# An attention and mixture-of-experts block: in the second half of the program, TensorE's products of one kind are put together

## What is computed

```python
x = x + _layernorm(_L0_attn_ref(_layernorm(x), Wq, bq, Wk, bk, Wv, bv))
x = x + _layernorm(_L0_ffn_ref(_layernorm(x), W_enc, ..., ln_g, ln_b))

# _L0_attn_ref
scores = jnp.einsum('bqh,bkh->bqk', q, k) / scale
probs = jax.nn.softmax(scores, axis=-1)
return jnp.einsum('bqk,bkh->bqh', probs, v)

# _L0_ffn_ref: D=128, H=256, M=64, E=8 experts, K=2 of them used, EH=128
spikes_enc = jax.nn.sigmoid(inputs_embeds @ W_enc + b_enc)
cont = flat @ W_s2c + b_s2c
probs = jax.nn.softmax(cont @ Wr + br, axis=-1)
topk_w, topk_idx = jax.lax.top_k(probs, K)
...
h = jax.nn.relu(jnp.einsum('tm,emh->eth', cont, W1) + b1[:, None, :])
y = jnp.einsum('eth,ehm->etm', h, W2) + b2[:, None, :]
expert_out = jnp.einsum('etm,te->tm', y, gate)
spikes_moe = jax.nn.sigmoid(expert_out @ W_c2s + b_c2s)
return _layernorm(spikes_moe @ W_dec + b_dec, ln_g, ln_b)
```

## Time and profile before

| | before |
|---|---|
| median of 3 runs | 129.09 us |
| the profiled execution | 128.96 us |
| its span, first to last instruction | 127.1 us |
| PE busy | 120.1 us, 94% |
| DVE busy | 91.7 us, 72% |
| ACT busy | 60.5 us, 48% |
| POOL busy | 34.7 us, 27% |

### The profile page before, as it was taken

One profiled execution on the slowest core, in us unless ns is written; L12 is line 12 of the kernel. 1 busy time (PEld: TensorE's weight loads), 2 busy tenths in 40 slices (PEclk: granted clock), 3 DMA queues, 4 the chain that ended last, 5 costly groups with the idle time before them and its releaser, 6 DMA issues.

```text
span 127.1 us, 2496 instructions
## 1 busy us (share of the span) xinstructions
PE 120.1 (94%) x814; PEld 80.0 (63%) x814; DVE 91.7 (72%) x390; ACT 60.5 (48%) x179; POOL 34.7 (27%) x71
## 2 busy tenths in 40 slices
PE   6999999999999999999999999999999999999940
PEld 2756785769638677755466776765548755864830
DVE  0858986996379625689765855899775986979873
ACT  1557765548646486303548662012552432281830
POOL 4422635232222003304000034402321311343361
PEclk9999999999999999999999999999999999999997
DMA  3548810000000039400000394002940029802022
GB/s 118 136 102 229 217 57 0 0 0 3 0 5 0 5 111 365 189 8 0 0 0 5 115 376 179 0 5 86 410 179 0 2 81 352 313 9 83 3 85 83
DMA packets 9371, 12.43 MB, mean 98 GB/s; under 512 B 3169, under 2 KB 5998, under 8 KB 9358
## 3 DMA queue, kind: packets, MB, share of 16 engines
q1 hardware_dynamic: 8782, 12.14, 27.9%
q10 hardware_dynamic: 576, 0.13, 0.5%
HBM read 11.16 MB, written 1.11 MB: 97 GB/s over the span
## 4 chain that ended last, share of the span: by engine, by line
PE 70%; DVE 11%; ACT 5%; DMA 4%; POOL 3%; issue 2%; POOLq 1%; SPq 0%; DVEq 0%
PE ps_o L826 11%; PE ps_s L801 10%; PE ps_t L934 7%; PE ps_t L813 5%; PE ps_s L913 4%; PE ps_ac L913 4%; POOL rstd L436 3%; PE ps_o L852 3%; DMA gate_all<-gates 3%; PE ps_ac L852 3%; PE ps_ac L774 2%; PE ps_ac L870 2%; PE ps_ac L784 2%; PE ps_t L752 2%; DVE gated L1304 2%
## 5 line engine op out<-in xcount | busy, mean ns | idle before, releaser
L436 POOL TENSOR_TENSOR rstd<-var_eps,minus_half 128x2 f32<-128x2 f32 (+1 forms) x32 | 24.9, 779 | 82.6 <-DVE var_eps L1188 41.3
L826 PEld LDWEIGHTS ps_o<-v,probsT 128*128 128x128 f32 x128 | 15.5, 192 | 4.8 <-ACT probsT L554 4.8
L826 PE MATMUL ps_o<-v,probsT 128*128 128x128 f32 x128 | 17.7, 281 | 0.3 <-ACT probsT L554 0.3
L934 PE MATMUL ps_t<-gated,w 128*64 128x256 f32 x128 | 17.1, 390 | 0.0
L549 ACT ACTIVATE probs<-ps_s,neg_max 128x512 f32<-128x512 f32 x16 | 11.0, 687 | 11.9 <-DVE neg_max L1211 11.8
L801 PE MATMUL ps_s<-xnT,yT 128*128 128x512 f32 x32 | 16.2, 600 | 0.0
L1211 DVE TENSOR_REDUCE neg_max<-ps_s 128x1 f32<-128x512 f32 x16 | 11.0, 690 | 5.5 <-PE ps_s L801 5.4
L934 PEld LDWEIGHTS ps_t<-gated,w 128*64 128x64 f32 x128 | 7.9, 136 | 7.4 <-DVE gated L1304 2.5
L1304 DVE SCALAR_TENSOR_TENSOR gated<-ps_s,b_minus,gate_all 128x512 f32<-128x512 f32 x14 | 10.0, 745 | 2.9 <-PE ps_s L913 2.2
L554 ACT ACTIVATE probsT<-ps_t 128x512 f32<-128x512 f32 x16 | 9.5, 594 | 2.6 <-PE ps_t L813 2.5
L813 PEld LDWEIGHTS ps_t<-ident,probs 128*128 128x128 f32 x64 | 7.3, 141 | 4.6 <-ACT probs L549 2.5
(11 more groups left out here) (203 smaller groups left out, 220.2 us busy)
## 6 DMA issues: line engine op xcount, KB each, us to landing
gate_all<-gates SPq DMA_DIRECT2D x12, 512.0 KB, 6.2
gate_all<-gates SPq DMA_DIRECT2D x8, 256.0 KB, 3.5
x_in<-in_L_attn_x SPq DMA_DIRECT2D x3, 256.0 KB, 3.6
w<-in_L_ffn_W SPq DMA_DIRECT2D x3, 256.0 KB, 4.3
out<-x_out SPq DMA_DIRECT2D x3, 256.0 KB, 2.0
x_in<-in_L_attn_x SPq DMA_DIRECT2D x2, 128.0 KB, 2.4
out<-x_out SPq DMA_DIRECT2D x2, 128.0 KB, 1.7
w_enc<-in_L_ffn_W_enc SPq DMA_DIRECT2D x1, 128.0 KB, 2.3
```

The lines of the kernel that those rows point to most:

```text
L436: nc.gpsimd.tensor_tensor(rstd[part], var_eps[part], minus_half[:, t0:t1], ALU.pow).then_inc(g_rstd[n], 1)
L826: mm = nc.tensor.matmul(attn_out(t), probsT[:, b % 2, t, k], v[:, b % 2, k], start=(k == 0), stop=(k == T - 1))
L934: mm = nc.tensor.matmul(ps_t[h * M:(h + 1) * M, 0:SH], w2[:, e], gated[:, e, h * SH:(h + 1) * SH], start=False, stop=(e == E - 1))
```

## The change

In the list of PE the work from batch 3's attention on is written in another order, so that products of one kind stand next to each other more often. `encode(2)` and `hidden_pair(1, 0)` go into batch 3's attention; `to_spikes(0)` goes behind it. The four tiles of a decode stand together, as do two pairs of hidden units and four or six expert sums. The lists of ACT and DVE follow. DVE's additions to the logits become two instructions for each batch, one for each bank; the logits of batch 2 lie in `ps_t` and `ps_a` in place of `ps_c`. Each expert sum raises `pe_moe` by one, so that `gate_hidden(b, e)` waits for the sum of the same expert of the batch before and no longer for all eight. One edit is earlier in the program: on ACT, `pT_out(1, 1)` goes ahead of `exps(1, 2)`. No product, activation or transfer is added or removed other than the four additions.

```diff
-        def logit_banks(b):
-            return ps_c if b in (0, 2) else ps_o
+        def logit_bank(b, h):
+            if b == 2:
+                return ps_a if h else ps_t
+            return (ps_o if b % 2 else ps_c)[:, h]
...
@@ ACT's list
+            pT_out(1, 1)
             exps(1, 2)
-            pT_out(1, 1)
...
@@ expert_out(b, e)
-                if e == E - 1:
-                    mm.then_inc(pe_moe, 1)
+                mm.then_inc(pe_moe, 1)
...
@@ PE's list, from the expert sums of batch 1 on
             hidden_pair(1, 1)
-            decode(0, 0)
-            decode(0, 1)
             hidden_pair(1, 2)
-            expert_out(1, 2)
-            expert_out(1, 3)
-            decode(0, 2)
-            decode(0, 3)
+            for t in range(T):
+                decode(0, t)
+            for e in range(2, 6):
+                expert_out(1, e)
             hidden_pair(1, 3)
...
             hidden_pair(2, 1)
             route(3)
-            decode(1, 0)
-            decode(1, 1)
-            expert_out(2, 2)
+            for t in range(T):
+                decode(1, t)
             hidden_pair(2, 2)
-            decode(1, 2)
-            decode(1, 3)
             hidden_pair(2, 3)
-            expert_out(2, 3)
-            expert_out(2, 4)
-            expert_out(2, 5)
+            for e in range(2, E):
+                expert_out(2, e)
             hidden_pair(3, 0)
-            expert_out(2, 6)
-            expert_out(2, 7)
             hidden_pair(3, 1)
             to_spikes(2)
             expert_biases(3)
+            expert_out(3, 0)
+            expert_out(3, 1)
             decode_part(2, 0)
             hidden_pair(3, 2)
-            expert_out(3, 0)
-            expert_out(3, 1)
             hidden_pair(3, 3)
...
@@ gate_hidden(b, e), DVE
-                if e == 0 and b >= 1:
-                    dve.wait_ge(pe_moe, b)
+                if b >= 1:
+                    dve.wait_ge(pe_moe, E * (b - 1) + e + 1)
...
@@ DVE's list, near the end
             dec_var(1, 0)
-            gate_hidden(3, 0)
-            gate_hidden(3, 1)
+            for e in range(4):
+                gate_hidden(3, e)
             z_scale(1, 0)
             z_stats(1, 0)
             z_means(1, 0)
-            for e in range(2, E):
+            dec_scale(2, 0)
+            for e in range(4, E):
                 gate_hidden(3, e)
-                if e == 3:
-                    dec_scale(2, 0)
```

More of the change, by code:

```diff
@@ L689, in _ @@
             pT_out(3, 0)
-            spike2(0, 0)
-            spike2(0, 1)
+            spike(2, 0)
             exps(3, 2)
@@ L993, in decode @@
                     pe.wait_ge(a_c2s, HC * (b + 1))
-                if t == 0:
-                    pe.wait_ge(a_cont, b + 3)
+                if b == 0 and t == 0:
+                    pe.wait_ge(v_logit, 2 * (B - 1))
+                elif t == 0:
+                    pe.wait_ge(a_cont, B)
                 last = any(t == t1 - 1 for _, t1 in parts(LN_DEC, b))
@@ L1101, in _ @@
             turn_h(2)
-            to_spikes(0)
             turn_probs(3, 0)
             scores(3, 2)
+            encode(2, 0)
             attend(3, 0)
@@ L1107, in _ @@
             scores(3, 3)
+            encode(2, 1)
             attend(3, 1)
             turn_probs(3, 2)
-            encode(2, 0)
+            hidden_pair(1, 0)
             attend(3, 2)
             turn_probs(3, 3)
-            encode(2, 1)
+            to_cont(2)
             attend(3, 3)
-            hidden_pair(1, 0)
-            to_cont(2)
+            route(2)
+            to_spikes(0)
             expert_biases(1)
             expert_out(1, 0)
-            route(2)
             expert_out(1, 1)
             hidden_pair(1, 1)
-            decode(0, 0)
-            decode(0, 1)
             hidden_pair(1, 2)
-            expert_out(1, 2)
-            expert_out(1, 3)
-            decode(0, 2)
-            decode(0, 3)
+            for t in range(T):
+                decode(0, t)
+            for e in range(2, 6):
+                expert_out(1, e)
             hidden_pair(1, 3)
-            expert_out(1, 4)
-            expert_out(1, 5)
             hidden_pair(2, 0)
+            turn_h(3)
             expert_out(1, 6)
             expert_out(1, 7)
-            turn_h(3)
+            encode(3, 0)
+            encode(3, 1)
             to_spikes(1)
             expert_biases(2)
-            encode(3, 0)
-            encode(3, 1)
             expert_out(2, 0)
@@ L1506, in _ @@
             attn_var(3, 0)
+            gate_hidden(1, 0)
+            gate_hidden(1, 1)
             mid_stats(3, 0)
-            gate_hidden(1, 0)
-            attn_var(3, 1)
-            gate_hidden(1, 1)
             router_top(2)
             router_index(2)
+            router_gates(2)
+            attn_var(3, 1)
             gate_hidden(1, 2)
-            gate_hidden(1, 3)
-            router_gates(2)
-            gate_hidden(1, 4)
-            gate_hidden(1, 5)
             mid_stats(3, 1)
+            for e in range(3, 6):
+                gate_hidden(1, e)
+            mid_norm(3, 0)
+            mid_norm(3, 1)
             gate_hidden(1, 6)
             gate_hidden(1, 7)
-            mid_norm(3, 0)
-            mid_norm(3, 1)
             dec_var(0, 0)
```

50 lines of the change are left out of this document (28 added, 22 removed).

## The result

The changed kernel took 130.78 us as the median of nine runs (129.95 to 132.9), the kernel before 129.06 us in as many. The ratio is 1.0121, with an interval from 1.0087 to 1.0155: slower by 1.7 us, where +0.4 to +0.5 was forecast and the range ended at 130.2. Its profiled execution took 129.97 us, with a span of 128.1 us, 1.0 us more than before, and a mean granted clock of 0.991. Eight of the nine runs form two groups: three at 129.95 to 129.98 us, with a mean clock of 0.990 to 0.993, and five at 130.56 to 131.25 us, with 0.977 to 0.982. Some executions of most kernels, that of 132.9 us among them, are slow, and in the three profiles of such a one PE's list is 1.5 to 1.6 us behind within 13 us of the start; the ratios leave them out, and from such a profile only intervals are read. So there are two things to explain: 1.0 us in the profile, and 0.6 to 1.3 us on top of it in most runs.

What follows compares the result with a forecast made beforehand. The end was taken to hang on when `z_scale(1)` starts on DVE, through POOL and ACT to the last gated units. +0.9 - 0.43 = +0.5 us gave 129.4 to 129.6, stated as 129.5 us; range 128.6 to 130.2.

Steps and rivals of the forecast that it cites:

- three signs of being wrong: `z_scale(1)` before 107.3; `gate_hidden(3, 2)` waiting for nothing or for PE; `route(3)` less than 1 us earlier.
- The marks in time: Starts near 26.75 for `turn_probs(1, 2)`, 95.1 `route(3)`, 98.9 unit behind `gate_blocks`, 108.0 `z_scale(1)`; last gated unit ending near 116.3.
- A change of kind at 0.18 us: On PE, each switch between kinds of product costs 0.18 us, bounds 0.16 and 0.20.
- the walk: PE's pieces up to `route(3)` laid end to end, looking for waits: 1.05 us gained; -1.0 taken.
- The first edit at -0.43: ACT's earlier `pT_out(1, 1)` lets `turn_probs(1, 2)` start earlier in batch 1's attention: -0.43 us, bounds -0.47 and -0.3.
- From `route(3)` to `z_scale(1)`: On DVE, `z_scale(1)` now waits for the third gate transfer and two gated units: +0.9 us before the first edit.
- its bound of +0.95 with 0.3 on top: Upper bound for `z_scale(1)`'s delay; 0.3 us more if `route(3)` gains only 0.8 or transfers take as long as batch 2's.
- Behind it nothing changes: After `z_scale(1)`, the statistics, power, `z_norm(1)`, `dec_square(2)`, `dec_var(2)` and last two gated units keep their order.
- the rival that has it fall: PE's clock drops to 1.2 GHz in the new gap before gated unit 6: 131.5 us, chance 0.04.
- The gain given up at the end: Seven later changes of kind saved on PE fall where PE waits, so 1.3 us is worth nothing.
- the first rival: All of PE's gain arrives: 12 changes at 0.18 and the early edit, -2.2 - 0.4, 126.5 us; chance 0.05.

Runs made afterwards that it cites:

- the late copy: Changed kernel with the early ACT edit undone, so `exps(1, 2)` again ahead of `pT_out(1, 1)`: 131.21 us, ratio 1.0156.
- the gated units alone: Kernel before, PE's order untouched, with only `gate_hidden(3, 2)` and `(3, 3)` put ahead of `z_scale(1)` on DVE: 131.74 us, ratio 1.0239.
- the gap filled: Changed kernel with eight bf16 products of zeros ahead of batch 3's last two expert sums: 129.79 us, and 129.73 us when repeated.
- the statistics first: Changed kernel with `z_scale(1)`, `z_stats(1)`, `z_means(1)` moved back ahead of `gate_hidden(3, 2)` and `(3, 3)` on DVE: 127.96 us, repeated 127.98 us.
- the two variants of it: Changed kernel with `z_scale(1)` and statistics behind `gate_hidden(3, 1)` and `dec_scale(1)` behind `gate_hidden(2, 7)`: 127.9 us; or with them ahead of all batch 3's gated units: 128.07 us.

## Why the prediction was right on the chain and wrong on the clock

The sign held, and so did the chain: `gate_hidden(3, 2)` was released by a `gate_all` landing, PE waited 2.08 us for the gated units, and `z_scale(1)` was later than before. None of the three signs of being wrong came, though `route(3)` only just passed (1.03 us earlier, with 1 as the mark). The marks in time came later than named, by 0.15 us at `turn_probs(1, 2)`, 0.4 at `route(3)` and at the gated unit behind `gate_blocks`, and 0.5 at `z_scale(1)` and at the last gated unit. What the prediction had wrong is the clock behind the gap. Point by point:

- **A change of kind at 0.18 us: right.** One side of a change still costs 0.10 us, and the stretch up to `route(3)` gave 0.87 us where 5 by 0.18 is 0.9, less the 0.1 of waiting that was laid out for `hidden_pair(1, 1)`; PE stood for 0.11. The 1.0 taken from the walk was 0.13 too much.
- **The first edit at -0.43: 0.1 too much.** The first 0.46 came as laid out (0.46 and 0.47 in two kernels). What failed is that all of 0.46 may go past the next transposes: the copy at 29.02, unmoved, let through 0.36, and 0.33 to 0.35 was left at batch 3's attention. The room was read as 30.12 less 29.61, 0.51 us, without the 0.14 us from the end of a copy to PE's start; with it, it is 0.37.
- **From `route(3)` to `z_scale(1)`: +1.19 for +0.93.** That is +1.03, with 0.33 for the first edit put back and 0.17 for the start taken off. The gates were out 0.81 us earlier, counted so, in place of 0.95. The third landing came 107.13 - 99.28 = 7.85 us behind the gated unit that follows `gate_blocks`, where 108.0 - 100.25 = 7.75 was taken from before. The rest is the 0.08 us from landing to DVE's start, taken as 0.05. The term was mis-sized, but its bound of +0.95 with 0.3 on top held it.
- **"Behind it nothing changes": right for the order, wrong for the clock.** In the profiled execution `z_scale(1)` is +1.03 and the span +1.0, so no wait behind it was overlooked. **The step that failed is that the products behind PE's new gap keep the full level of the clock.** The sum puts nothing for it, and the rival that has it fall got a chance of 0.04. A mean clock of 0.982 or less, which goes with the longer times, stands in 13 of 22 runs of the three kernels that have the gap: eight of 13 of the changed one, three of five with the late copy, two of four with the gated units alone. In the 20 runs with the gap filled, in the 51 of the other variants, whose profiles show no wait of PE over 0.95 us behind its first products, and in all repeats of the kernel before, the mean was 0.988 or more.
- **Why the chance was so small.** The prediction has the gap as "twice what it stood before". Before, PE did not stand for 1 us there: its last sums lost 0.29 us in all to waits (3.10 us against 2.81). A gap of 0.3 us had become one of 2.08. The trace of before has no such gap in the middle of PE's work (its waits are of 0.3 us each, but for 1.2 ahead of the first product), so its full clock "as long as PE worked" could not speak for or against a fall behind 2 us.
- **The rival's price was too high for this kernel.** 131.5 was laid out for it, 2 us above the forecast. Measured, a fallen clock adds 0.6 to 1.3 us in the changed kernel and 1.6 to 1.9 where only the gated units were moved. The products of "the last 5 us" were to run slowly; the one trace shows the low level for some 3.4.
- **The gain given up at the end: right.** The later changes saved on PE lie in the time in which it waits. With the statistics first, they still bring little: the kernel gains 1.1 us, which is about the 0.35 of the first edit and the 0.87 up to `route(3)`, less 0.1, and not the 2.6 of the first rival. One wait on the way was not laid out, 0.60 us at 102.63 for gated unit 6 of batch 2; the third landing covers it.

Put together: `z_scale(1)` came 0.5 us later than forecast, 0.26 from its own term, 0.10 from the first edit and 0.17 from the start of this execution, and the profiled execution took 129.97 us, half a microsecond over the forecast and inside the range. The fallen clock took the median to 130.78, outside it.

The best version is the changed kernel with the statistics first: 127.96 and 127.98 us on two chips, 1.1 us under the kernel before and 2.8 under the changed one; the two variants of it, at 127.9 and 128.07, can't be told from it. What stays open is why the clock fell in some executions of one and the same kernel and not in others. The profiles in which it didn't fall have gaps of 1.98, 2.07 and 2.08 us, the one in which it fell 2.23; one such profile is too few to say that the length decides.

## What to carry to other kernels

Before work is put ahead of a long chain on an in-order engine, ask what its own inputs wait for: two gated units of 1.4 us that need a late transfer cost 2 us more ahead of a chain over DVE, POOL and ACT than behind its first part. A saving on a busy engine reaches the end only as far as the next transfer or chain lets it, so take it from the last wait backwards and not from a count. Where a change opens a gap of some 2 us on TensorE in the middle of its work, price the slow clock behind it as a likely case (here it took more than half of the runs), and ask first whether the trace before has a gap of that length at all; then look at the mean clock of each run, and fill the gap with products on zeros to see what it costs.

## What the runs showed of the hardware that I had not expected

The granted clock can fall for a gap that isn't at the end of the work: after 2.23 us without products it went to 0.50 for some 3.4 us (all of 120 to 122, and 0.68 on the mean of 122 to 124), beginning only some 1.7 us after PE had started again (PE worked from 118.21, the clock fell a little before 120). By the mean clock of the runs the same kernel did so in some executions and not in others, 8 of 13 for the changed one, which gave its times two groups. Eight useless bf16 products, 1.9 us in all, kept the level in 20 of 20 runs and were worth 1.0 us. And the third transfer of the gates landed 7.75 us behind the start of the gated unit that follows the gates in the kernel before, and 7.7 to 8.0 us in the six other profiles in which DVE waited for it.
